# Softmax-weighted values with the keys stationary: u arrives transposed, and its sums are inverted by way of DMA

## The reference

```python
x = x + tanh(g_xattn) * xattn(layernorm(x), ctx)      # 16 heads of 64
x = x + tanh(g_ffn)   * ffn(layernorm(x))             # 32 experts, 8 of them per token, and a shared one

# xattn, per batch (128 queries, 128 keys of 64 features) and head
scores = (xn @ Wq_h) @ (ctx @ Wk_h).T / 8
out_h  = softmax(scores) @ (ctx @ Wv_h)
xattn  = concat(out_h) @ Wo + bo

# ffn
w   = top-8 of sigmoid(xn @ gate_w.T) + gate_bias within the 2 best of 4 groups, normalised, * 2.5
ffn = sum_e w_e * (silu(xn @ G_e) * (xn @ U_e)) @ D_e  +  shared(xn)
```

## Time and profile before

| | |
|---|---|
| median of 3 runs | 703.02 us (702.43 to 705.61) |
| the profiled execution, its own time | 703.62 us |
| its span | 701.8 us, mean granted TensorE clock 0.995 |
| busy: TensorE / VectorE / ScalarE / GpSimd | 683.8 / 512.6 / 331.3 / 266.2 us |
| attention, about | 30 to 384 us of the span |
| experts, about | 389 to 702 us of the span |

### The profile page before, as it was taken

The page is one execution under the profiler, slowest core; times in us unless marked ns, Lnnn a source line. Parts: engine busy times, 40 slices in busy tenths (PEclk is TensorE's granted clock), DMA queues, the critical chain, the costliest instruction groups (busy, mean ns, idle before and its releaser), DMA issues.

```text
span 701.8 us, 15942 instructions
## 1 busy us (share of the span) xinstructions
PE 683.8 (97%) x4700; PEld 580.8 (83%) x4700; DVE 512.6 (73%) x1640; ACT 331.3 (47%) x627; POOL 266.2 (38%) x316
## 2 busy tenths in 40 slices
PE   8799999999999999999999898999999999999997
PEld 6589889888889889889998686878787888878785
DVE  6775877768767777687567596877778686969565
ACT  3243344434443344434344555555555555555553
POOL 4212121222122121212310264656666565756654
PEclk9999999999999999999999999999999999999999
DMA  5401000000000000000000554535363636455550
GB/s 134 131 19 27 17 19 18 22 18 18 18 18 18 19 17 18 24 18 18 18 2 1 115 131 95 136 90 138 86 160 79 165 91 155 106 124 136 111 148 15
DMA packets 44815, 47.27 MB, mean 67 GB/s; under 512 B 11744, under 2 KB 27232, under 8 KB 44768
## 3 DMA queue, kind: packets, MB, share of 16 engines
q1 hardware_dynamic: 44768, 46.72, 27.4%
HBM read 43.81 MB, written 2.62 MB: 66 GB/s over the span
## 4 chain that ended last, share of the span: by engine, by line
PE 89%; POOL 4%; issue 4%; DVE 1%; DMA 1%; ACT 0%; POOLq 0%; SPq 0%; DVEq 0%
PE bank L1105 16%; PE bank L1029 13%; PE bank L1031 13%; PE bank L1030 13%; PE bank L1137 8%; PE bank L1065 5%; PE bank L1113 5%; POOL halves L457 4%; PE bank L1085 3%; PE bank L1091 2%; PE bank L1088 2%; PE bank L1094 2%; PE bank L1152 1%; PE bank L1036 1%; PE bank L1075 1%
## 5 line engine op out<-in xcount | busy, mean ns | idle before, releaser
L457 POOL TENSOR_TENSOR halves<-area,halves 128x512 fp32r<-128x512 f32 x135 | 174.6, 1293 | 145.0 <-ACT halves L580 139.4
L537 ACT ACTIVATE area<-bank 128x512 f32<-128x512 f32 x128 | 69.5, 595 | 190.7 <-PE bank L1094 190.7
L593 ACT ACTIVATE area<-bank 128x512 f32<-128x512 f32 x136 | 81.3, 597 | 112.6 <-PE bank L1031 111.8
L989 DVE TENSOR_TENSOR bank<-area,bank 128x512 f32<-128x512 f32 x128 | 88.6, 692 | 55.4 <-PE bank L1031 54.7
L1105 PE MATMUL bank<-ctx_keys,area 128*128 128x65 f32 x1024 | 123.1, 271 | 0.0
L1105 PEld LDWEIGHTS bank<-ctx_keys,area 128*128 128x128 f32 x1024 | 120.6, 192 | 0.4 <-issue 0.4
L1029 PE MATMUL bank<-x2t_hi,w_hi 128*128 128x512 f32 x272 | 110.4, 406 | 2.2 <-DVE area L997 2.1
L1031 PE MATMUL bank<-x2t_lo,w_hi 128*128 128x512 f32 x272 | 107.0, 393 | 0.0
L710 DVE TENSOR_REDUCE row_max<-bank 128x4 f32<-128x512 f32 x128 | 82.0, 684 | 33.5 <-PE bank L1065 28.9
L1030 PE MATMUL bank<-x2t_hi,w_lo 128*128 128x512 f32 x272 | 106.5, 392 | 0.0
L405 POOL TENSOR_TENSOR ctx_hi<-ctx_raw,ones_col 128x128 fp32r<-128x128 f32 x32 | 12.8, 400 | 238.7 <-PE bank L1094 232.2
(11 more groups left out here) (119 smaller groups left out, 1099.0 us busy)
## 6 DMA issues: line engine op xcount, KB each, us to landing
wbc<-rows_dram SPq DMA_DIRECT2D x128, 256.0 KB, 4.4
w_raw<-experts SPq DMA_DIRECT2D x32, 102.0 KB, 2.0
ctx_raw<-ctx_t SPq DMA_DIRECT2D x64, 32.0 KB, 2.1
out<-area SPq DMA_DIRECT2D x7, 256.0 KB, 4.2
ctx_keys<-ctx_nat SPq DMA_DIRECT2D x32, 32.0 KB, 1.8
max_rows<-max_t SPq DMA_DIRECT2D x64, 4.0 KB
area<-wq_t SPq DMA_DIRECT2D x1, 512.0 KB, 4.6
area<-wo SPq DMA_DIRECT2D x1, 512.0 KB, 4.4
```

Source lines behind the costliest of these rows:

```text
L457: nc.gpsimd.tensor_tensor(hid_lo[:, u % SLOTS, :], hid[:, u % HIDS, :], raw(hid_hi[:, u % SLOTS, :]), ALU.subtract).then_inc(hidlo_ready, 1)
L537: nc.scalar.activation(probs_t[:, k, :, :], st_ps[q][:].rearrange("p (h n) -> p h n", h=4), ACT.Exp)\
L593: nc.scalar.activation(silu_g[:, u % 2, :], gate_ps[u % 2][:], ACT.Silu).then_inc(silu_ready, 1)
L989: nc.vector.tensor_tensor(up_ps[u % UPS][:], silu_g[:, u % 2, :], up_ps[u % UPS][:], ALU.mult)\
```

## The change

`weigh` swaps its operands: the context is stationary and the probabilities of four heads are streamed, 512 columns at once. u comes out with features on partitions and queries along the row, as the projection wants it. The even head's keys are followed by the column of ones (65 columns: u on partitions 0 to 63, its sums in row 64), the odd head's are preceded by it (128 columns: sums in row 0, u on 64 to 127). `transpose_u` is gone.

```diff
-                for i in range(4):
-                    ins = nc.tensor.matmul(u_ps[q][:, i * (CD + 1):(i + 1) * (CD + 1)],
-                                           probs_t[:, k, i, :], ctx_keys[:, b, :], start=True, stop=True)
-                ins.then_inc(u_done, 1)
-            def transpose_u(t, parity, r): ...
+                keys = ctx_keys[:, b, 0:CD + 1] if q == 0 else ctx_keys[:, b, CD:3 * CD]
+                nc.tensor.matmul(u_ps[q][0:CD + 1 if q == 0 else P, :], keys,
+                                 probs_t[:, k, :, :].rearrange("p i n -> p (i n)"), start=True, stop=True).then_inc(u_done, 1)
```

The sums now lie along a row. ScalarE copies u and its sums to SBUF (`u_out`, four per batch in place of two `ut_out`). SyncE spreads the 2 x 1024 sums over 128 partitions x 16, VectorE takes one reciprocal, SyncE writes the result to DRAM and reads it back broadcast over 64 partitions for each q:

```diff
+            def spread_sums(t, parity):
+                wait_first(u_ready, 4 * t + 4)
+                for q in range(2):
+                    row = CD if q == 0 else 0
+                    sp.dma_start(sums[rows(q), parity, :], u_raw[parity][row:row + 1, q, :, :]).then_inc(sums_in, 16)
+            def store_inverse(t, parity):
+                wait_first(inverse_ready, t + 1)
+                sp.dma_start(inverse_dram[parity]..., inverse[:, parity, :]).then_inc(inverse_out, 16)
+            def spread_inverse(t, parity):
+                wait_first(inverse_out, 16 * t + 16)
+                for q in range(2):
+                    wait_first(norm_ready[q], t)
+                for q in range(2):
+                    sp.dma_start(inverse_bc[rows(q), :, :]..., inverse_dram[parity, q:q + 1, :].broadcast_to([HD, 2 * CT])).then_inc(inverse_in, 16)
+            def invert(t, parity):
+                dve.wait_ge(sums_in, 32 * t + 32)
+                wait(dve, inverse_out, 16 * (t - 1))
+                nc.vector.reciprocal(inverse[:, parity, :], sums[:, parity, :]).then_inc(inverse_ready, 1)
```

Then `u_t = u_raw * inverse_bc`, 64 partitions x 1024: `normalise_even` on GpSimd, `normalise_odd` on VectorE. `project_out` and `residual` lag three batches instead of two. The orders of the engines in iteration t:

```diff
 SyncE:
+                    load_max_row(t + 1, (b + 1) % 2, t - 1)
                     load_raw(b, (t + CB) * P)            # one DMA in place of two
                     load_weights(b % 2, (t + 2) * WSTEP)
-                    load_max_row(t + 1, (b + 1) % 2, t - 1)
                     load_keys((b - 1) % CB, t - 1 + CB)  # writes the keys twice, around the ones
+                    spread_sums(t - 1, (b - 1) % 2)
+                    store_inverse(t - 1, (b - 1) % 2)
+                    spread_inverse(t - 1, (b - 1) % 2)
 VectorE, at the end of each half h:
-                        for q in range(2): normalise(...)
+                        if h == 0:
+                            normalise_odd(t - 2, b % 2)
+                            invert(t - 1, (b - 1) % 2)
 GpSimd:
                     add_bias(t, c)
+                    normalise_even(t - 2, b % 2)
                     split_context(b, t + CB, c + 1)
```

More of the change, by code:

```diff
@@ L320, in attention @@
                     t = CB * c + b
+                    if not (last and b == CB - 1):
+                        load_max_row(t + 1, (b + 1) % 2, t - 1)
                     if not last:
@@ L331, in attention @@
                         load_keys((b - 1) % CB, t - 1 + CB)
+                    if not (first and b == 0):
+                        spread_sums(t - 1, (b - 1) % 2)
+                        store_inverse(t - 1, (b - 1) % 2)
+                        spread_inverse(t - 1, (b - 1) % 2)
             in_chunks(sp, attention)
@@ L439, in attention @@
                     add_bias(t, c)
+                    if last and b == CB - 1:
+                        x2t_low(0, 0)
+                    if not (first and b < 2):
+                        normalise_even(t - 2, b % 2)
                     if not last:
@@ L460, in experts_low @@
                         x2t_low(c + 1, 1 - parity)
-            x2t_low(0, 0)
+                    if first and u == NORM_AT:
+                        normalise_even(NB - 1, (NB - 1) % 2)
+            normalise_even(NB - 2, NB % 2)
             in_all_chunks(experts_low)
@@ L548, in attention @@
                     if not (first and b == 0):
-                        ut_out(t - 1, (b - 1) % 2, 0)
+                        for q in range(2):
+                            u_out(t - 1, (b - 1) % 2, 1, q)
+                    if last and b == CB - 1:
+                        x2t_out(1, ut_ps)
                     if b == 1:
@@ L573, in _ @@
             in_chunks(act, attention)
-            for r in range(2):
-                ut_out(NB - 1, (NB - 1) % 2, r)
+            for q in range(2):
+                u_out(NB - 1, (NB - 1) % 2, 1, q)
             def hidden_high(c, u):
@@ L601, in experts_of @@
                         y_out(c - 1)
-                    if routed_at(c, u, 0):
+                    if routed_at(c, u, 0) and not first:
                         x2t_out(c + 1)
@@ L911, in attention @@
                                 take_max(t + 2, b % 2, h, q)
-                        if h == 1 and not (first and b < 2):
-                            residual(t - 2)
+                        if h == 1 and not (first and b < 3):
+                            residual(t - 3)
                         if not last:
@@ L929, in attention @@
                                 route_chunk_0(SEAM[1], SEAM[2])
-                        for q in range(2):
-                            if h == 1:
-                                if q == 1 and b % 2 == 1 and not last:
-                                    g_low(2 * c + 2 + b // 2, b // 2)
-                                normalise(t, b % 2, 0, q)
-                            elif not (first and b == 0):
-                                normalise(t - 1, (b - 1) % 2, 1, q)
+                        if h == 1 and b % 2 == 1 and not last:
+                            g_low(2 * c + 2 + b // 2, b // 2)
                         if step_of_chunk == 2 and not last:
@@ L1199, in attention @@
                     if last and b == CB - 1:
-                        pe.wait_ge(x2_ready, t - 2)
-                    if not (first and b < 2):
-                        project_out(t - 2, b % 2, t + 1 if last and b == CB - 1 else t + 2)
+                        pe.wait_ge(x2_ready, t - 3)
+                    if not (first and b < 3):
+                        project_out(t - 3, (b + 1) % 2, t + 1 if last and b == CB - 1 else t + 2)
                     if not (last and b >= 2):
```

186 lines of the change are left out of this document (101 added, 85 removed).

## The result

The changed kernel takes 745.65 us (742.29 to 749.14, 4 runs) beside 704.32 (702.43 to 706.71, 4 runs): a ratio of 1.0585, with an interval of 1.0521 to 1.065. It is slower by 41 us. The profiled execution took 746.94 us, its span is 745.2 and its mean granted clock 0.972; that span is 43.4 above the one before.

What follows compares the result with a forecast made beforehand. TensorE was taken as the bound, newly made to wait for maxima behind the sums' chain. Profiled 703.6 + 44.7 (chain, TensorE's saving included) - 3 (seam) + 5 (clock) = 750.3, predicted 750 us; 8 in 10 range 712 to 795.

Steps and rivals of the forecast that it cites:

- TensorE's own work: Attention iteration on TensorE: transposes gone, weigh 0.14 us less; 1.07 us less each, even 8.81, about 33 us over 31 iterations.
- The chain: Sums' DMA through SyncE, then VectorE's reciprocal ahead of the maxima: even iterations +1.38 us, odd +1.92, or +1.5 with b = 1.
- The sum of the loop: Attention loop: 14 even iterations at +1.38, 7 odd at +1.92, 8 odd at +1.5, together +44.7 us.
- The clock: Low clock level after TensorE's gaps at odd iterations' starts: +0.74 us each, counted for half of 15, +5 us.
- The first and last iterations: Chain counted from t = 1 to t = 29, at the same cost per even or odd iteration as elsewhere.
- The seam: Last two iterations and passage to the experts: -3 us, between -6 and +2.
- the two late projections: The last two projections, at the seam, only move into the experts.
- the faster one: Rival: sums land in time and TensorE waits for nothing, about 668 us; 17%.
- The clock's rival: Every TensorE gap is followed by the low clock level, 34 us in place of 5, about 779 us; 15%.
- rival 3: GpSimd's and VectorE's products take turns in SBUF, 2.6 + 2.5 us, +15 us in the odd iterations, about 765 us; 8%.

Runs made afterwards that it cites:

- no sums: Changed kernel without the two DMAs that spread the sums and the reciprocal's wait for them, the sums a constant: 683.0 us, ratio 0.969.
- sums first: Changed kernel with SyncE issuing the sums' DMA directly behind the row of maxima, ahead of raw, weights and keys: 698.11 us, ratio 0.9909.
- both on VectorE: Kernel with the sums issued first, plus the even heads' product moved from GpSimd to VectorE, behind the odd heads' one: 700.35 us, ratio 0.9949.
- VectorE first: Kernel with the sums issued first, plus a wait so GpSimd's product starts only when VectorE's is done: 699.78 us, ratio 0.9934.
- both on GpSimd: Kernel with the sums issued first, plus the odd heads' product moved from VectorE to GpSimd: 711.52 us, ratio 1.0103.
- odd product later: Kernel with the sums issued first, plus VectorE's normalise_odd moved behind the maxima and the residual in odd iterations: 710.95 us, ratio 1.01.
- idle products: Changed kernel plus two 512-column f32 matmuls that nobody reads at the start of each odd iteration: 755.98 us, ratio 1.0737.

## Why the prediction was right

The forecast was 750, the time is 745.65, and it came by the mechanism written down. That it came within 5 us is in part luck, since several terms missed in opposite directions. By its steps, in us from the start of the traced iteration at 307.94:

- *TensorE's own work*: right. Four `weigh` records take 311.52 - 309.80 = 1.72, 0.43 each, as worked out. Where nothing else waits, an even iteration is 8.7 to 8.9 (no sums, sums first); predicted 8.81.
- *The chain*: first row of maxima 3.38 (predicted 3.39), raw 5.09 (5.19), weights 5.70 (5.81), keys 6.38 (6.43), sums 6.88 (7.05), reciprocal 9.48 (9.67), next start 11.08 (11.26). TensorE's wait is 2.11 (2.45), and at the g projection 329.39 - 319.02 = 10.37 (10.65), a wait of 2.44. The unknown form, one partition to many, landed 1.9 us behind its issue in the median (1.7 at the least, 3.0 at the most); I had taken 1.8.
- *The sum of the loop*: by SyncE's cuts the twelve pairs of the six chunks grew by 3.28 us each; by the prediction's +1.38 and the mean of +1.92 and +1.5 they should by 3.09. But 0.55 of the 3.28 is the clock (next item). The chain itself brought 2.73, less than predicted: +1.2 in an even iteration (10.88 against 9.69), +2.0 with b = 3 (14.86 against 12.85), and only +1.1 with b = 1 (14.24 against 13.15), where I had counted +1.5.
- *The clock*: the right place and the right price, but too seldom. Even iterations, measured from one row of maxima to the next and so with the start of the odd one behind them, take 10.87 to 10.90 in three of twelve cases and 11.0 to 12.3 in the nine where the low level follows the gap: 6.6 us in all, 0.73 for each of the nine. Predicted were 0.74 and every second one, 4.4 us for these twelve. In the windows below TensorE stands from 212.8 to 214.9, and 0.50, the 1.2 GHz level, follows.

```profile
212.00:214.00 2.00, 0.81 (x2) 0.00 (x0) 0.72 (x2) 1.22 (x3) 1.56 (x3) 1.00 0.04 3
214.00:216.00 2.00, 1.11 (x12) 1.04 (x14) 1.31 (x4) 0.00 (x0) 0.00 (x0) 0.83 0.05 4
216.00:218.00 2.00, 2.00 (x10) 1.05 (x7) 1.85 (x8) 0.46 (x1) 0.00 (x0) 0.50 0.74 188
218.00:220.00 2.00, 2.00 (x6) 0.85 (x5) 1.10 (x10) 1.35 (x4) 0.00 (x0) 0.81 0.34 74
```

- *The first and last iterations*: over-sized. Of the +44.7 some 37 fall on the six chunks (twelve pairs) and 7.6 on the five iterations around them; these brought 1.6 (+0.5 and +1.1). From t = 0 to 2 the kernel after needs 14.41 us where before it took 18.02, as two rows of maxima go out together; from t = 2 to 3 it loses 3.9 (15.74 against 11.88); and from t = 30 on nothing waits for the maxima any more.
- *The seam*: -3 was forecast, and the stretch from the row of t = 31 to the end became 1.4 longer, within the range given (-6 to +2). It is 1.5 shorter up to the first product that needs the routed weights (399.52 - 365.39 = 34.13 before, 440.01 - 407.40 = 32.61 after), though five transposes of about 0.47 and one projection of 1.9 left it: TensorE's idle time in it grew from 3.5 to 5.4 us, with new waits of 1.38 (for `u_out`) and 2.47 (for VectorE's routing of chunk 0, the line below), and a clock of 0.95 took more. Behind that point it is 2.9 longer, where I had counted that the two late projections, 1.9 us each, only move. The step that failed is this one: they moved from a stretch that partly waits into one that TensorE fills. The misses of these two items, -6.0 and +4.4, hid each other.

```profile
430.72 1.01 PE L1186 MATMUL bank<-ident,weight 128*32 128x128 f32 x4 [2.47 <-DVE weight L922]
```

The rivals: the faster one would have needed the sums at about 5, and the run without sums comes to 683, 15 above its 668. The clock's rival had the low level behind every gap: it followed nine of twelve at the starts of odd iterations and none ahead of the g projections there (the last section has one). GpSimd and VectorE do get in each other's way, as rival 3 had it: VectorE's product of 1.22 us took up to 3.42, GpSimd's of 2.35 too. It had the pair too long (2.6 + 2.5 us; started together they are done after 3.4), and it was wrong in where that lies: in the changed kernel it falls in VectorE's wait for the sums (309.95 to 313.26, with the sums in at 317.3) and costs nothing; once the sums are early it is the next thing in line. The Trainium skill's "GPSIMD Engine Reference", § Specifications, names the shared SBUF interfaces; the traces agree, and they add that VectorE's instructions of 4 elements per partition are held too (1.55 us in the timeline above, 2.34 at the most).

The sums' median landing of 1.9 us is close to the 2.0 of the Trainium skill, "DMA: Bandwidth & Descriptors", § Anatomy of one DMA; by that 2.0 the forecast would have been 756. The section is written for DMAs issued by GpSimd, though, and all of these are issued by SyncE, so the prediction leaned on it further than it reaches.

Not settled: what holds the odd iterations of the kernel with the sums first at 12.8 to 14.2. Taking the contention off one place moved the time by nothing (both on VectorE, VectorE first) or cost (both on GpSimd, odd product later). By iterations the picture is sharper: those with b = 1 got shorter in all four runs (on average 13.0 to 13.2 us in the first two, 12.3 to 12.5 in the others, 13.7 with the sums first), those with b = 3 got longer (13.9 to 14.9 against 13.6); in the timelines of b = 3 `g_low` was late in the product's stead. A kernel that treats the two kinds differently was not tried. That VectorE, ScalarE and GpSimd are in sum too late for g with b = 3 fits all four runs; it wasn't tested by itself.

## What to carry to other kernels

When work leaves the engine that bounds a kernel, write down the whole way that its replacement takes, in the order of each in-order engine, and ask what is queued behind each new wait: here an estimated 33 us saved on TensorE turned into 41 us lost, since a DMA issued fifth instead of second reached a reciprocal that stood ahead of the maxima. Issue the transfer on whose result an engine stands before those that are needed an iteration later; an issue costs 0.5 to 0.7 us on SyncE, and each is paid in full on such a path. A wait that is removed uncovers what it hid: before moving an instruction out of a wait, look at what ran in its shadow.

## What the runs showed that was not expected

- A VectorE product and a GpSimd product of 64 x 1024 in SBUF take turns rather than share. Between 30 and 430 us they overlap 212 times in the traces of the changed kernel and of eight experiments. Whichever starts first runs at its own pace (1.22 or 2.35 us), even where its lead is 0.04 us or less; the other ends 1.1 us (VectorE's) or 2.2 us (GpSimd's) behind it, a little less than its own length, up to 3.45 us from its start. One VectorE product of the 212 took 0.35 longer.
- VectorE's steps of 4 elements per partition took up to 2.34 us beside a GpSimd product (both products on GpSimd), against 0.16 or 0.17 alone, and one that reads a single tensor was held no less than one that reads two.
- Filling one gap of TensorE moved the low clock to the next one, ahead of the g projection. The length of that gap alone doesn't decide. With the idle products the low level followed all six gaps of 2.1 to 2.7 us in the six chunks, but only two of the six gaps of 1.72 to 1.74. In the changed kernel the same place has gaps of up to 2.69 us, and the clock stayed at 1.00 behind all of them, as behind the 2.44 us at 329.39 (windows below). What decides these runs do not tell.

```profile
328.00:330.00 2.00, 0.61 (x5) 0.61 (x6) 1.53 (x4) 0.01 (x1) 1.57 (x4) 1.00 0.05 4
330.00:332.00 2.00, 2.00 (x20) 2.00 (x19) 1.67 (x10) 1.39 (x3) 0.21 (x1) 1.00 0.00 0
```
